# Storing a matmul's stationary blocks pairwise interleaved, with the moving operand left in place

## The reference

```python
# x (64, 64, 1024), one condition number of 16 per batch row
W = cond_weights[condition]                      # (64, 64, 64)
y = einsum('bct,bcd->bdt', x, W)                 # (64, 64, 1024)
gate_logits = y @ gate_w.T                       # 8 experts
weights, selected = top_k(gate_logits, 2); weights = softmax(weights)
result = y @ base_w.T + base_b                   # 1024 -> 1024
low = y @ lora_A[e].T                            # rank 16 per expert
result += 2.0 * sum_e w_full[e] * (low[e] @ lora_B[e].T)
out = x + result
```

## Time and profile before

| | us |
|---|---|
| median of three runs | 494.29 |
| the profiled execution, its own time | 494.55 |
| its span, first to last instruction | 492.5 |
| TensorE matmuls busy | 487.7 (99%) |
| weight loads busy | 480.8 (98%) |
| ACT busy | 382.2 (78%) |
| DVE busy | 371.0 (75%) |
| GpSimd busy | 128.5 (26%) |
| DMA, mean rate | 89 GB/s |

### The profile page before, as it was taken

The page is one execution under the profiler, slowest core; times in us unless marked ns, Lnnn a source line. Parts: engine busy times, 40 slices in busy tenths (PEclk is TensorE's granted clock), DMA queues, the critical chain, the costliest instruction groups (busy, mean ns, idle before and its releaser), DMA issues.

```text
span 492.5 us, 8737 instructions
## 1 busy us (share of the span) xinstructions
PE 487.7 (99%) x2771; PEld 480.8 (98%) x2771; DVE 371.0 (75%) x800; ACT 382.2 (78%) x740; POOL 128.5 (26%) x111
## 2 busy tenths in 40 slices
PE   8999999999999999999999999999999999999997
PEld 8999999999999999999999999999999999999997
DVE  5988877778787778787787877787877787777653
ACT  4898878878778887788787788887788877887620
POOL 2033202333113333033232223332133320233130
PEclk9999999999999999999999999999999999999999
DMA  8812122221221221221222222212212212211112
GB/s 333 352 43 80 69 91 89 61 95 58 91 91 58 91 96 51 91 92 53 96 63 82 89 79 70 96 53 91 91 55 96 87 59 88 96 53 55 56 43 85
DMA packets 31986, 43.89 MB, mean 89 GB/s; under 512 B 18402, under 2 KB 22498, under 8 KB 31970
## 3 DMA queue, kind: packets, MB, share of 16 engines
q1 hardware_dynamic: 31826, 43.17, 25.0%
q10 hardware_dynamic: 144, 0.52, 0.4%
HBM read 25.00 MB, written 18.68 MB: 89 GB/s over the span
## 4 chain that ended last, share of the span: by engine, by line
PE 91%; DMA 3%; ACT 3%; DVE 1%; SPq 1%; issue 0%; ACTq 0%
PE acc L642 76%; PE acc L674 9%; PE mixed L662 5%; DMA x_sb<-in_x 3%; ACT y_moved L363 1%; ACT x_parts L350 1%; SPq L219 1%; DVE w_raw L467 0%; ACT w_raw L355 0%; DVE w_raw L548 0%; DVE w_raw L551 0%; SPq L215 0%; DVE y_turned L474 0%; DVE y_lo L481 0%; ACT y_hi L386 0%
## 5 line engine op out<-in xcount | busy, mean ns | idle before, releaser
L642 PE MATMUL acc<-w_hi,y_hi 128*128 128x384 f32 (+1 forms) x768 | 257.3, 338 | 0.5 <-ACT w_hi L336 0.3
L642 PE MATMUL acc<-w_lo,y_hi 128*128 128x384 f32 (+1 forms) x768 | 257.0, 338 | 0.0
L642 PE MATMUL acc<-w_hi,y_lo 128*128 128x384 f32 (+1 forms) x768 | 256.6, 337 | 0.0
L363 ACT COPY y_moved<-w_raw 32x256 f32<-32x256 f32 x480 | 194.1, 404 | 38.0 <-DVE w_raw L467 32.3
L295 POOL TENSOR_TENSOR w_raw<-x_sb,bias 128x1024 f32<-128x1024 f32 x32 | 77.2, 2414 | 345.4 <-DVE low L522 277.7
L642 PEld LDWEIGHTS acc<-w_hi,y_hi 128*128 128x128 f32 x768 | 144.0, 188 | 4.0 <-DVE w_raw L548 0.7
L642 PEld LDWEIGHTS acc<-w_lo,y_hi 128*128 128x128 f32 x768 | 143.9, 188 | 2.5
L642 PEld LDWEIGHTS acc<-w_hi,y_lo 128*128 128x128 f32 x768 | 144.0, 188 | 0.0
L467 DVE TENSOR_TENSOR w_raw<-mixed,w_raw 64x1024 f32<-64x1024 f32 x60 | 73.0, 1217 | 30.0 <-ACT w_raw L355 29.6
L474 DVE STREAM_TRANSPOSE y_turned<-y_moved 128x512 f32<-128x512 f32 x60 | 42.3, 706 | 51.2 <-ACT y_moved L363 51.2
L355 ACT COPY w_raw<-mixed 64x1024 f32<-64x1024 f32 x60 | 60.7, 1012 | 20.9 <-PE mixed L662 20.1
(11 more groups left out here) (52 smaller groups left out, 239.7 us busy)
## 6 DMA issues: line engine op xcount, KB each, us to landing
x_sb<-in_x SPq DMA_DIRECT2D x32, 512.0 KB, 3.3
out<-w_raw SPq DMA_DIRECT2D x31, 512.0 KB, 2.6
w_raw<-in_proj_w SPq DMA_DIRECT2D x8, 580.0 KB, 9.5
scratch<-low_squares SPq DMA_DIRECT2D x29, 64.0 KB, 1.5
lowT_raw<-scratch SPq DMA_DIRECT2D x116, 16.0 KB, 1.7
cw<-in_cond_w ACTq DMA_DIRECT2D x1, 512.0 KB, 3.6
lb_raw<-in_lora_b SPq DMA_DIRECT2D x1, 512.0 KB, 16.4
bias<-in_base_b SPq DMA_DIRECT2D x1, 512.0 KB, 17.1
```

The source lines that it names most:

```text
L363: done = nc.scalar.copy(y_moved[q * SQ:(q + 1) * SQ, g, :, :], piece.rearrange("m (k q a) -> m q k a", q=QUARTERS, a=SQ)[:, q, :, :])
L642: return nc.tensor.matmul(acc[:, c % 2, b, 0:hi - lo], y_part[:, c % 2, k, :], w_part[:, k, lo:hi], start=(k == 0 and product == 0), stop= ...
```

## The change

`y_hi` and `y_lo` change their layout in a partition. Before, block k of 128 columns was contiguous: 512 bytes, 4 bytes from column to column. Now blocks 2i and 2i + 1 share 1024 bytes, and their columns alternate: column m of the even block, column m of the odd block, column m + 1 of the even block. So the stationary operand of a projection matmul is read with 8 bytes from column to column. The sizes of the tensors and their places stay as they were. The instructions that write `y_hi` and `y_lo` write at 8-byte steps, and the subtraction also reads `y_hi` so. `y_turned` is now stored block by block (4-quarter order inside a block), so that its readers go through each block in runs of 128 columns; the turn writes runs of 32 columns 128 columns apart in each block row. The split weights `w_hi` and `w_lo` stay where they are, with rows 4640 bytes apart. No instruction is added, removed or moved: the order on every engine, the waits, the shapes and the DMAs are those of the kernel before.

```diff
-        y_turned = sb("y_turned", [P, QUARTERS, KT, SQ], F32)
-        y_hi = sb("y_hi", [P, 2, KT, P], F32R)
-        y_lo = sb("y_lo", [P, 2, KT, P], F32R)
+        y_turned = sb("y_turned", [P, KT, P], F32)
+        y_hi = sb("y_hi", [P, 2, HALF_K, P, 2], F32R)
+        y_lo = sb("y_lo", [P, 2, HALF_K, P, 2], F32R)
...
+        def y_block(part, c, k):
+            return part[:, c % 2, k // 2, :, k % 2]
+
+        def y_half(part, c, h):
+            return part[:, c % 2, h * HALF_K // 2:(h + 1) * HALF_K // 2].rearrange("p i m e -> p i e m")
+
         def turned_half(h):
-            return y_turned[:, :, h * HALF_K:(h + 1) * HALF_K, :].rearrange("p g k m -> p k g m")
+            return y_turned[:, h * HALF_K:(h + 1) * HALF_K, :].rearrange("p (i e) m -> p i e m", e=2)
+
+        def mixed_half(h):
+            return mixed[:, h, :].rearrange("p (i e m) -> p i e m", e=2, m=P)
...
-                high = y_hi[:, c % 2, h * HALF_K:(h + 1) * HALF_K, :].rearrange("p k (g m) -> p k g m", m=SQ)
-                nc.scalar.copy(high, turned_half(h)).then_inc(y_hi_ready, 1)
+                nc.scalar.copy(y_half(y_hi, c, h), turned_half(h)).then_inc(y_hi_ready, 1)
...
-                nc.vector.transpose(y_turned[:, :, ks, :], y_moved[:, :, ks, :]).then_inc(turned, 1)
+                nc.vector.transpose(y_turned[:, ks, :].rearrange("p k (g m) -> p g k m", m=SQ), y_moved[:, :, ks, :]) \
+                    .then_inc(turned, 1)
...
-                nc.vector.tensor_tensor(low_part, turned_half(h), high, ALU.subtract).then_inc(y_ready, 1)
+                nc.vector.tensor_tensor(y_half(y_lo, c, h), turned_half(h), y_half(y_hi, c, h).bitcast(F32),
+                                        ALU.subtract).then_inc(y_ready, 1)
...
-                return nc.tensor.matmul(acc[:, c % 2, b, 0:hi - lo], y_part[:, c % 2, k, :], w_part[:, k, lo:hi],
+                return nc.tensor.matmul(acc[:, c % 2, b, 0:hi - lo], y_block(y_part, c, k), w_part[:, k, lo:hi],
```

More of the change, by code:

```diff
@@ L339, in y_high_first @@
                 act.wait_ge(mix_done, 2 * c + h + 1)
-                nc.scalar.copy(y_hi[:, c, h * HALF_K:(h + 1) * HALF_K, :],
-                               mixed[:, h, :].rearrange("p (k m) -> p k m", m=P)).then_inc(y_hi_ready, 1)
+                nc.scalar.copy(y_half(y_hi, c, h), mixed_half(h)).then_inc(y_hi_ready, 1)
             def x_high(j, c, first=False):
@@ L450, in y_low_first @@
                 dve.wait_ge(y_hi_ready, 2 * c + h + 1)
-                ks = slice(h * HALF_K, (h + 1) * HALF_K)
-                nc.vector.tensor_tensor(y_lo[:, c, ks, :], mixed[:, h, :].rearrange("p (k m) -> p k m", m=P),
-                                        y_hi[:, c, ks, :].bitcast(F32), ALU.subtract).then_inc(y_ready, 1)
+                nc.vector.tensor_tensor(y_half(y_lo, c, h), mixed_half(h), y_half(y_hi, c, h).bitcast(F32),
+                                        ALU.subtract).then_inc(y_ready, 1)
             def x_low(j, c, b):
@@ L473, in turn @@
                 ks = slice(h * HALF_K, (h + 1) * HALF_K)
-                nc.vector.transpose(y_turned[:, :, ks, :], y_moved[:, :, ks, :]).then_inc(turned, 1)
+                nc.vector.transpose(y_turned[:, ks, :].rearrange("p k (g m) -> p g k m", m=SQ), y_moved[:, :, ks, :]) \
+                    .then_inc(turned, 1)
             def y_low(j, c, h):
                 dve.wait_ge(y_hi_ready, 8 * j + 2 * c + h + 1)
-                ks = slice(h * HALF_K, (h + 1) * HALF_K)
-                high = y_hi[:, c % 2, ks, :].bitcast(F32).rearrange("p k (g m) -> p k g m", m=SQ)
-                low_part = y_lo[:, c % 2, ks, :].rearrange("p k (g m) -> p k g m", m=SQ)
-                nc.vector.tensor_tensor(low_part, turned_half(h), high, ALU.subtract).then_inc(y_ready, 1)
+                nc.vector.tensor_tensor(y_half(y_lo, c, h), turned_half(h), y_half(y_hi, c, h).bitcast(F32),
+                                        ALU.subtract).then_inc(y_ready, 1)
             def rank_gates(j, c):
```

## The result

The changed kernel takes 497.33 us (median of four runs, 497.00 to 497.93) against 494.33 for the kernel before (four runs): ratio 1.0063, 95% interval 1.0046 to 1.0081. It is slower by 0.6%. The forecast was 491.1, faster. The profiled execution took 497.17 with a span of 495.1; before, 494.55 and 492.5.

What follows compares the result with a forecast made beforehand. TensorE's matmul distance was taken as the bound. Writes and the rest at zero, stationary reads 3.2 us off: 494.55 became 491.35, and with the median 0.26 lower, 491.1 us; forecast's own range 487.9 to 493.3, whole range 487.9 to 500.7.

Steps and rivals of the forecast that it cites:

- What bounds the kernel: TensorE, busy 99% of 492.5 us at 2.4 GHz: time is number of matmuls times the distance between their starts.
- The writes at zero, the slack as cover: ACT and DVE writing y at 8-byte steps: zero cost, with 0.63 us of slack before the next step's first load.
- The load does not become the bound at 8 bytes: Projection's weight loads: may take 1.5 times as long for nothing; load-bound rival at twice, 134 us more, 628, chance 0.05.
- The 0.10 us per step "over the experts' pace", read as clashes: Projection: 12.66 us against 12.56 at the experts' pace, the excess read as y's fetch clashing with w's streaming.
- 3.2 us to win: Projection's stationary reads: 8-byte steps would remove most of 0.10 us in each of 32 steps; forecast's chance 0.45.
- Two streams at one speed either keep clear of each other or meet once: Projection: 8-byte loads match w's streaming speed, so a stream held up stays clear; most of 0.10 us per step goes.
- The rival on the other side: Projection loads: twice the clashes, 0.20 us per step instead of 0.10, 3.2 us more, 497.5; chance 0.22.
- its second form: Equal speed locks some blocks into a repeating clash through w's rows at 4640 bytes; also 497.5, two doublings 500.7.
- Its first form: Loads span 1024 bytes instead of 512, touching twice as many pieces of memory, each with its chance of a clash; 497.5.
- The rival "no change": Projection: block differences come from w's rows alone, y's place has no part; 494.3, chance 0.18.
- The two-port rule: Skill's rule on TensorE: loading next weights takes no read bandwidth from the running matmul; by it 494.3.

Runs made afterwards that it cites:

- by_four: Four blocks of y interleaved, 16 bytes from column to column, same computation, against the kernel before: 628.07 us, ratio 1.2695.
- writes_only: The changed kernel, but TensorE reads 128 contiguous columns of the interleaved storage: 494.58 us, ratio 0.9997 to the kernel before.
- one_column: The kernel before with a stationary operand that repeats its first column 128 times: 493.48 us, one run.
- both_32_inter: The changed kernel with w's rows 4864 bytes apart, w's rows and y both moved by 32 bytes: 494.39 us, ratio 0.9994 to the kernel before.

## Why the prediction was wrong

- **What bounds the kernel: right.** Only the distance between matmuls' starts counted, in every run; in `by_four` it was the load that set this distance.
- **The writes at zero, the slack as cover: right.** ACT's cast became 51 ns longer, and the slack of 0.63 us took it; `writes_only` equals before.
- **The load does not become the bound at 8 bytes: right.** Its price at twice the time was confirmed at 16 bytes; where between the two it starts to bind was not tested.
- **The 0.10 us per step "over the experts' pace", read as clashes: the step that failed first.** I took the blocks' distances above the experts' for lost time, and the experts' for a floor. With rows at 4864 and at 4672, and with one row for all, the blocks' times were different, and the step stayed at 14.973 us in each: long distances in one place were made up by short ones elsewhere, in part in the mix and the experts' matmuls. The experts' pace is no floor either, since their nine matmuls took from 1.393 to 1.412 us in kernels that don't touch them. There was no 3.2 us to win: contiguous loads were already as good as anything tried but `one_column` (0.026 us a step, 0.8 us in the run).
- **"Two streams at one speed either keep clear of each other or meet once": the step that gave the wrong sign.** The loads at 8-byte steps did become sensitive to the relation with the streamed rows, as two streams at one speed might; that the speeds are equal now is still my estimate, since no row gives the load's own speed. But in every relation tried other than 0 it costs, up to 0.19 us a step. With rows 4640 bytes apart the blocks run through eight different relations, and only one of them is the good one, 0: 0.094 us a step where I had -0.10.
- **The rival on the other side** named 497.5, and its second form (the equal speed locks some blocks into a clash that repeats, and w's rows, left at 4640 bytes, put them there) is what the runs bear out, so far as it speaks of place; the clash itself is inferred. Its first form, twice the stretch of memory and so twice the clashes, does not hold: the stretch is the same in `both_32_inter`, which loses nothing. That the size fits to 0.2 us is chance, since it was built on the 0.10 that was no clash.
- **The rival "no change"** had the cause of the unequal blocks right: with one row of w for all, contiguous blocks take 1.577 to 1.583 us. It was wrong that the place of y has no part once the load reads at 8-byte steps.
- **The two-port rule** that I weighed there (the Trainium skill, "TensorE: Matmul & The Clock Gate", step-by-step part: loading doesn't take read bandwidth from the running matmul) agrees with contiguous loads within 0.1% of a step as the place of w changes (14.973 to 14.987). It does not account for loads at 8-byte steps, where w's place alone moves the time from 494.84 to 499.54.

**What stays open.** That streaming and loading meet in some piece of the memory is inferred from the dependence on their relation; no row shows such a meeting. The whole shape of the dependence was not found: the eight relations of the change average out at 15.067, and 96, 160 and 192 were not tried one by one. Why contiguous loads lose 0.047 us a step when both w and y are moved, where interleaved ones lose nothing, is open too, and so is what makes up for the blocks' differences within a step.

## What to carry to other kernels

Before you read unequal distances of equal matmuls as lost time, compare a whole period of the program: here they were redistributed, and no placement tried made the whole step shorter. A stationary operand at 8-byte steps did not make the load the bound, but its cost then depends on how it lies in memory relative to the moving operand (0 to 1.2% here), so if a layout needs such steps, give the moving rows a common place modulo 256 bytes that agrees with the stationary blocks' place. At 16-byte steps of float32 the load takes twice its time, and ACT and DVE here took 1.8 and 1.6 times theirs.

## What the runs showed that I had not expected

- The length of a step takes only certain values. The steps of all kernels in which the load was not the bound were 14.947, 14.973, 14.980, 14.987, 15.020, 15.033, 15.040, 15.060, 15.067, 15.140 and 15.167 us, and all differences are multiples of about 6.7 ns (16 cycles at 2.4 GHz, worked out) within the 1 ns of the records. Why is open. The mean of the load's record went up by about as much, from 188 to 194 or 195 ns. Six kernels, with five different placements of TensorE's operands among them, had exactly 14.973.
- ACT's cast feels the new layout (622 to 673 ns for 128x512), DVE's subtraction does not (692 to 693). The order in which both read `y_turned` changed with the step of the output; in `by_four` the output alone went on to 16 bytes and ACT to 1143 ns, which points to the output.
- A load that repeats one address has the same record (188 ns) as one of 128 contiguous columns.
